# Graph network on one core: setup phases merged, first count-table edges and first feature rows made earlier, issues of weights and x moved

## What is computed

```python
h = maximum(layernorm(x), 0)
feat = einsum('ni,rhid->rnhd', h, conv_weights)             # 8 types: 2048 columns per node
e = leaky_relu(el[type, src] + er[type, dst], 0.2)          # el, er = sum(feat * attn_l / attn_r)
x = x + segment_sum(softmax_per_dst(e) * feat[type, src]) + h_bias
h = maximum(layernorm(x), 0)
h = h @ W_in + b_in
for l in range(3):
    agg = segment_sum(h[src], dst) / deg
    h = relu(agg @ W_agg[l] + h @ W_self[l] + b_hid[l])
x = x + h @ W_out + b_out
```

## Time and profile before

| what | value |
|---|---|
| median of 3 runs | 2069.59 us (2069.22 to 2075.5) |
| the profiled execution: own time, span | 2072.4 us, 2070.6 us |
| busy share of the span | PE 86%, PE weight load 60%, ACT 55%, DVE 52%, POOL 25% |
| mean granted TensorE clock | 0.901 |
| setup, up to the build stage's first one-hot | 0 to 156.6 us |
| build stage, up to the last quarter's store | 156.6 to 529.1 us |
| first gather | 533.0 us |

### The profile page before, as it was taken

The page is one execution under the profiler, slowest core; times in us unless marked ns, Lnnn a source line. Parts: engine busy times, 40 slices in busy tenths (PEclk is TensorE's granted clock), DMA queues, the critical chain, the costliest instruction groups (busy, mean ns, idle before and its releaser), DMA issues. The chain is left out here.

```text
span 2070.6 us, 26209 instructions
## 1 busy us (share of the span) xinstructions
PE 1778.8 (86%) x7604; PEld 1236.5 (60%) x7605; DVE 1081.7 (52%) x3126; ACT 1143.4 (55%) x2498; POOL 521.1 (25%) x544
## 2 busy tenths in 40 slices
PE   1159999999497879798797955999989999999998
PEld 1054444444375557565575634777777777877777
DVE  4858888888365676766767535453550000301011
ACT  0034455565387779797787734454545444544442
POOL 2600000000577777777777300000000000000000
PEclk7569999999687789797898887999999999999999
DMA  4314555555655566565665325333324333363432
GB/s 129 82 14 152 171 195 192 181 201 199 202 146 161 152 182 176 153 188 159 171 173 161 101 63 181 99 123 107 110 77 128 113 116 112 98 208 123 135 123 62
DMA packets 285221, 290.67 MB, mean 140 GB/s; under 512 B 88673, under 2 KB 248102, under 8 KB 284806
## 3 DMA queue, kind: packets, MB, share of 16 engines
q1 hardware_dynamic: 235094, 186.23, 29.3%
q0 software_dynamic: 23952, 66.46, 12.1%
q10 hardware_dynamic: 26016, 36.15, 4.8%
HBM read 201.26 MB, written 87.48 MB: 139 GB/s over the span
## 5 line engine op out<-in xcount | busy, mean ns | idle before, releaser
L1141 POOL DMA_INDIRECT work<-feat_tab,fidx_i x499 | 477.6, 957 | 586.0 <-issue 581.2
L2117 PE MATMUL PS<-a_pe,y_hi 128*128 128x512 f32 (+2 forms) x1440 | 556.7, 392 | 33.4 <-ACT a_pe L2014 33.4
L2117 PE MATMUL PS<-a_pe,y_lo 128*128 128x512 f32 (+2 forms) x1440 | 536.7, 379 | 0.0
L2014 ACT ACTIVATE a_pe<-a_in 128x1536 fp32r<-128x1536 f16 (+1 forms) x240 | 329.3, 1376 | 342.7 <-PE PS L2117 329.1
L2117 PEld LDWEIGHTS PS<-a_pe,y_hi 128*128 128x128 f32 (+1 forms) x1440 | 274.0, 190 | 103.1 <-ACT a_pe L2014 35.0
L1210 ACT ACTIVATE work<-work 128x64 f32<-128x64 f32 x1344 | 325.1, 332 | 0.0
L2117 PEld LDWEIGHTS PS<-a_pe,y_lo 128*128 128x128 f32 (+1 forms) x1440 | 274.2, 190 | 55.2 <-issue 6.7
L1385 PE MATMUL PS<-work,stg 128*128 128x260 f32 x1008 | 289.6, 437 | 6.5 <-ACT work L1210 4.6
L1385 PEld LDWEIGHTS PS<-work,stg 128*128 128x128 f32 x1008 | 207.5, 217 | 65.0 <-issue 19.6
L255 DVE TENSOR_SCALAR side<-iota_c,work 128x512 f16<-128x512 f16 x705 | 245.8, 349 | 0.0
L1325 PE MATMUL PS<-wbuf,hT 128*128 128x512 f32 x480 | 226.9, 595 | 0.0
(11 more groups left out here) (257 smaller groups left out, 1674.0 us busy)
## 6 DMA issues: line engine op xcount, KB each, us to landing
a_in<-a_tab SPq DMA_DIRECT2D x210, 384.0 KB, 3.2
feat_tab<-stg ACTq DMA_DIRECT2D x120, 260.0 KB, 2.2
a_tab<-side SPq DMA_DIRECT2D x235, 128.0 KB, 1.8
stg<-dst_tab SPq DMA_DIRECT2D x42, 384.0 KB, 4.0
work<-feat_tab,fidx_i POOLq DMA_INDIRECT x499
h_tab<-outs SPq DMA_DIRECT2D x42, 130.0 KB, 2.6
h_tab<-outs SPq DMA_DIRECT2D x8, 520.0 KB, 3.9
stg<-h_tab SPq DMA_DIRECT2D x8, 520.0 KB, 4.1
```

The costliest lines, as they stand in the source:

```text
L1141: pool.indirect_dma_start(out=ring[:, s, 0:FE], out_offset=None, in_=feat_tab[:, :], in_offset=bass.IndirectOffsetOnAxis(ap=idx, axis=0)). ...
L2014: act.activation(a_pe[:, load % A_PE, :, 0:n], a_in[:, load % A_IN, :, 0:n], ACT.Copy).then_inc(s_conv, 1)
L2117: mm = pe.matmul(SUMS(ug, n)[:, f, :], y[0:rows_of, kb, f * P:(f + 1) * P], a_pe[0:rows_of, load % A_PE, kb % KB, 0:n], start=(kb == 0 and ...
```

## The change

It has six parts.

- The weights' issues leave the first phase: eight for each half of K, on ACT and on SP, in the phase of tile ends. The attention vectors (ACT) and x with the four small vectors (SP) go into the check phase.
- The products for `wlr` go to the end of the tile tables' lists of DVE and POOL.
- The window phase and the norm phase are one. DVE makes `edge_i` first, behind only the four L749-like instructions and their 28 matmuls, then runs the norm, and then the rest of the window chain. SP starts `load_pairs` when `edge_i` is there, then stores `er_tab`, then `rm_tab`.
- PE and ACT make the 12 quarters of the first `AHEAD` = 3 blocks in this phase, behind the norm.
- The build stage has 27 blocks (3 to 29) for the same 235 windows, so 8 or 9 each; `EARLY` is 8.
- Buffers: the index rows no longer lie in `hT` (an own tile `index_rows`), `hN` and `hTs` lie in `side`, `elr` has its own tile, x's last block is zeroed in the first phase (and again only if a sort ran).

```diff
+AHEAD = 3
+BLOCK_W = [0] * AHEAD + [NREAL * (b + 1) // (NBLK - AHEAD) - NREAL * b // (NBLK - AHEAD) for b in range(NBLK - AHEAD)]
-EARLY = 10
+EARLY = 8
...
+        def load_weights(eng, k):
+            for r in range(R):
+                eng.dma_start(wc[:, k, r * F:(r + 1) * F].rearrange("p (h d) -> p h d", h=H),
+                              conv_w[r, :, k * P:(k + 1) * P, :].rearrange("h p d -> p h d")).then_inc(s_at, 16)
...
+                if flag is None:
+                    @block.scalar
+                    def _(act):
+                        load_weights(act, 0)
+
+                    @block.sync
+                    def _(sp):
+                        load_weights(sp, 1)
...
+            @block.scalar
+            def _(act):
+                load_attention(act)
+
+            @block.sync
+            def _(sp):
+                load_nodes(sp)
...
+                    if flag is None:
+                        attention_sums(dve)
...
+                c.link(dve.tensor_scalar(small[0:1, 35:36], small[0:1, 27:28], float(P), None, ALU.mult))
+                dve.wait_ge(s_we, 1)
+                c.link(dve.tensor_scalar(edge0, PS[0:1, 7, 0:NTW], float(GRAIN), None, ALU.mult))
+                c.link(dve.tensor_scalar(edge0, edge0, small[0:1, 35:36], None, ALU.min))
+                c.link(dve.tensor_copy(edge_i[:, :], edge0))
+                dve.sem_inc(s_wd, 1)
+                dve.wait_ge(s_xr, 1)
+                ln_stats(dve, x_rows(0), 0, 0, s_bs, s_vr)
+                over_chunks(dve, step)
...
                 over_chunks(act, step)
+                act.wait_ge(s_ee, NC)
+                for q in range(4 * AHEAD):
+                    keep_features(act, q)
...
                 halves(NC - 1, (NC - 1) % 2)
+                pe.wait_ge(s_ht, 2 * NC)
+                for cc in range(4):
+                    sum_features(pe, cc)
+                pe.wait_ge(s_ee, NC)
+                for c in range(CT):
+                    pe.matmul(PS[0:1, 5, 0:NTW], one_c, ended[:, PARTS_T - 1, c, :], start=(c == 0), stop=(c == CT - 1))
+                pe.wait_ge(s_w, PARTS_T + 7)
+                for c in range(CT):
+                    mm = pe.matmul(PS[0:1, 6, 0:NTW], ones[:, 0:1], begun[:, c, :], start=(c == 0),
+                                   stop=(c == CT - 1))
+                mm.then_inc(s_wc, 1)
+                for q in range(4, 4 * AHEAD):
+                    sum_features(pe, q)
...
-                for b in range(EARLY):
+                sp.wait_ge(s_wd, 1)
+                for b in range(AHEAD, AHEAD + EARLY):
                     load_pairs(sp, b)
                 over_chunks(sp, store)
+                sp.wait_ge(s_ri, 12)
+                at = 0
+                for a, n in ((csx, U + 1), (cbx, U), (cnx, U)):
+                    for h in range(H):
+                        sp.dma_start(rm_tab[:, at:at + n].unsqueeze(0), a).then_inc(s_rw, 16)
+                        at += n
+                sp.wait_ge(s_rw, 16 * 3 * H)
                 sp.wait_ge(s_et, 16 * NC)
```

More of the change, by code:

```diff
@@ L742, in _, with x_rows, keep, step @@
             def _(dve):
-                dve.memset(x_all[:, NBLK - 1:32, :], 0.0).then_inc(s_xz, 1)
+                def x_rows(c):
+                    return lambda b: x_all[:, bass.ds(c * 4 + b, 1), :].rearrange("p o f -> p (o f)")
+                def keep(c, slot):
+                    dve.wait_ge(s_el, c + 1)
+                    dve.tensor_scalar(elr[:, bass.ds(c * 4, 4), :, :],
+                                      PS[:, 4 + slot, 0:256].rearrange("p (b i n) -> p b i n", b=4, i=2),
+                                      0.0, None, ALU.add).then_inc(s_ee, 1)
+                def step(c, slot, first, last):
+                    if not last:
+                        ln_stats(dve, x_rows(c + 1), c + 1, 1 - slot, s_bs, s_vr)
+                    if not first:
+                        wait_past(dve, s_tp, c - 1)
+                    ln_finish(dve, x_rows(c), c, slot, s_sd, s_rs, s_hn, hN[:, slot, :, :])
+                    if not isinstance(c, int) or c > 1:
+                        keep(c - 2, slot)
+                with when(dve, 0):
+                    dve.memset(x_all[:, FULL:32, :], 0.0).then_inc(s_xz, 1)
                 c = Chain(dve, s_w)
@@ L976, in step @@
                         halves(c - 1, 1 - slot)
+                for g in range(PARTS_T):
+                    pe.wait_ge(s_w, g + 2)
+                    for c in range(CT):
+                        mm = pe.matmul(PS[0:1, 7, 0:NTW], one_c, ended[:, g, c, :], start=(g == 0 and c == 0),
+                                       stop=(g == PARTS_T - 1 and c == CT - 1))
+                mm.then_inc(s_we, 1)
                 over_chunks(pe, step)
                 halves(NC - 1, (NC - 1) % 2)
+                pe.wait_ge(s_ht, 2 * NC)
[5 more added lines that the diff above has]
+                pe.wait_ge(s_w, PARTS_T + 7)
+                for c in range(CT):
+                    mm = pe.matmul(PS[0:1, 6, 0:NTW], ones[:, 0:1], begun[:, c, :], start=(c == 0),
[3 more added lines that the diff above has]
+                    sum_features(pe, q)
             @block.sync
@@ L983, in _ @@
                 sp.wait_ge(s_ld, 16 * 4)
+                sp.wait_ge(s_xl, 32)
+                with when(sp, 0):
+                    load_all_x(sp, 2)
+                    sp.wait_ge(s_xl, 64)
+                sp.sem_inc(s_xr, 1)
                 def store(c, slot, first, last):
@@ L1171, in _ @@
                 w = 0
-                for b in range(NBLK):
+                for b in range(AHEAD, NBLK):
                     for cc in range(4):
-                        q, slot = 4 * b + cc, cc % 2
                         for _ in range(BLOCK_W[b] // 4 + (cc < BLOCK_W[b] % 4)):
@@ L1315, in _ @@
                 w = 0
-                for b in range(NBLK):
+                for b in range(AHEAD, NBLK):
                     for cc in range(4):
-                        q = 4 * b + cc
                         for _ in range(BLOCK_W[b] // 4 + (cc < BLOCK_W[b] % 4)):
```

253 lines of the change are left out of this document (106 added, 147 removed).

## The result

The changed kernel took 2080.94 us (median of 11 runs, 2078.8 to 2091.34); the kernel before took 2074.26 beside it (11 runs, 2063.84 to 2078.3). The ratio is 1.005, with a 95% interval of 1.0032 to 1.0068: it is slower by half a per cent. The forecast of 2054.7, "faster" and the range of 2043 to 2066 are all wrong.

What follows compares the result with a forecast made beforehand. It took setup lists (no engine full) and, in the build stage's loaded part, PE and SP equally full, as the bounds. Gains of 0.9 (setup) and 14 (build stage) made 14.9: span 2055.7, from the median 2054.7 us, range 2043 to 2066.

Steps and rivals of the forecast that it cites:

- the term of the build stage: Build stage: 12 quarters gone and 27 blocks in place of 30, gain taken as 14 us.
- lower bound: Build stage: loaded stretch grows with the windows, 255.1 to 269.8 us; stage 367.6, gain 5.
- upper bound: Build stage: PE sets the pace with the same 14.5 us over, gain 20.5.
- The one for slower: Build stage: longer register loads lengthen SP's list, up to 36.7 us added, 2091; chance 0.04.
- The build stage as the windows go: Build stage at the lower bound, 2064 us; chance 0.15 together with a front 8 us later.
- Quarters at half clock: Merged phase: quarters at 3.42 us in place of 1.71, phase ends with PE, 2072, no change; chance 0.07.
- The lateness goes away: Build stage: pair loads no longer disturb it, 31 us gained, 2038; chance 0.05.
- the four signs of being wrong: Tile ends stretched to 17 us; x's issue held up; merged-phase quarters 3.4 apart; ACT's `a_tab` wait well beyond 57.6.
- First phase and tile ends: Setup: first phase 7.1 us shorter, then eight weight issues on each of ACT and SP, 8.5, end 20.9.
- Check: Setup: SP's issues of x and vectors become the longest list, 11 us (bounds 9.5 and 16), end 31.9.
- Tile tables: Setup: DVE's own 13.7 us as before, then products 16.0, end 66.3, next phase at 68.4.
- Merged phase: Setup: `edge_i` at 81.3, SP's list ends last at 148.4, build stage's first DVE instruction at 153.6, 0.9 us gained.

Runs made afterwards that it cites:

- eight_slots: Changed kernel with eight slots in place of four for window evictions, in a tile of their own: 2249.66 us in one run, build stage 343.2.
- fixed addresses: Changed kernel, pair loads in turn with constant addresses, no register loads (the choice of right edges left out): 2039.71 us in one run, stage 342.8.
- two bursts: Changed kernel with each block's pair loads half at its head, half in its middle: 2045.8 us in one run, stage 345.4.
- in turn: Changed kernel with SP issuing one pair load, one window store, and so on: 2046.75 us, 0.985 of before.
- best: Changed kernel with x's large issue last, loads and stores in turn, POOL's first product held until s_te 6: 2038.68 us, 0.9839 of before.
- interleaved kernel before: Kernel before with pair loads between window stores and nothing else: 2264.45 us, 0.9946 of before on the second chip, stage 361.4.

## Why the prediction was wrong, point by point

**The step that failed: the term of the build stage** ("I take 14", between a lower bound of 5 and an upper of 20.5); the stage grew by 2.8 us where this term took 14 away. It made a sum of SP's list, 250.3, and one of PE's, 237.2, and treated the 14.8 over the sum as a lateness that shrinks.

The sum of SP's list was wrong in itself. Its 0.81 for a window store is the length of a row in which SP also waits for ACT's evictions: 46.8 us of such waits, 48 times, lie in the loaded part of before. Where nothing is waited for, a store comes each 0.50 us (the row of `eight_slots`). By that price the change's list is 166 x 0.50 + 165 x 0.50 + 19 x 2.5 = 213 us, an estimate, and well under PE's 237. SP was not the longer list, and interleaved, the same list let the stage run at PE's pace. What binds is the time in which no window store is issued, against what ACT's slots cover. A quarter with two windows takes 3.01 us, so ACT wants a slot each 1.5 us and four slots are some 6.0 us. This is an estimate; it counts neither the 1.8 us (median) from a store's issue to its landing nor the windows in flight.

The gaps without a store at the blocks' heads, from SP's rows of each trace:

| | gap at a head: median (range) | heads over the cover | cover | stage |
|---|---|---|---|---|
| before | 6.8 (5.0 to 8.7) | 14 of 19 | 6.0 | 372.3 |
| after | 7.7 (5.3 to 10.4) | 16 of 18 | 6.0 | 375.1 |
| fixed addresses | 4.4 (3.9 to 7.1) | 3 of 18 | 6.0 | 342.8 |
| two bursts (the second: 2.7) | 4.9 (3.3 to 7.7) | 6 of 18 | 6.0 | 345.4 |
| in turn | 3.5 (1.7 to 5.4) | none | 6.0 | 344.1 |
| eight slots | 7.9 (5.8 to 10.3) | none | 12.0 | 343.2 |

The four edits work at different places and give the same stage, within 2.6 us: the cause is shown. The 6.0 itself is no sharp edge. With two bursts six heads were over it and PE waited for ACT once, 1.4 us; with fixed addresses three were, and it didn't wait. That goes with the 4 us of ACT's stall that PE does not feel. What gives PE these 4 us, its banks in PSUM ahead of ACT most likely, no run varied. PE's floor by the forecast's own prices is 235 x 0.65 + 108 x 1.71 = 337.4.

The kernel before was already at the edge, and interleaving it gave 11 us. The change took 12 quarters out, but kept every window and made blocks longer: nine loads in a burst in place of eight, and a median gap of 7.7 in place of 6.8. PE's waits for ACT went from 8.4 us to 22.7 by it, as 11 of ACT's 17 stalls were now longer than 4 us (the longest 8.5, before 6.1).

The lower bound was wrong for the same reason: "the stretch goes with the windows" gives 269.8, the profile 278.1. A bound scaled by windows has no term for a burst that gets longer. And of the upper bound, 20.5, the stage without the burst gives 17.3 to 18.8 (361.4 and 362.1 to 344.1 and 343.3), so that number was nearly right, for a kernel in which SP's stores come in time.

**A wrong number in it**: the register load of 1.77 was a median over two phases. Ten of its 30 are in the norm, where they are shorter; the 20 of the stage have a median of 2.32, and 2.55 after the change:

```profile
L215 SPq TENSOR_LOAD <-edge_i x20: 549/2322/3700, 156.8 to 399.1; - x20
```

**The rivals.** The one for slower named SP's list at the block's head, and set its point at a mean register load of 2.55. It was the right place, and the mean in the stage was 2.51; but its working, a sum of extra microseconds added to a list, was that of the failed step, and by it 2.5 would have given no more than "the gain is gone". "The build stage as the windows go" named ACT's waits for SP's stores as what speaks for it: that was the cause, under-weighted. "Quarters at half clock" is refuted for the merged phase: the issues of its quarters come 1.59 to 1.83 apart, but for the gap of 5.56, and the clock was 1.00 from 125 to 153. Half clock came in the build stage, where nobody looked for it, and cost 8 us there. "The lateness goes away" was given 0.05 with the note that SP has more to do per block; it does, and with the loads in turn the lateness goes away all the same. Of the four signs of being wrong two were met: x's issue was held up, and ACT's wait for `a_tab` stores grew to 80.6.

**The setup**, 4.5 us off, as four terms:

- First phase and tile ends: right or better. The landing came 3.0 after the last issue (bounds 2 to 5.7). The 16 issues of weights took 5.8 us on two queues, not 8.5, where one queue had taken 16.92 amid other traffic. But both figures are lengths of issue lists. The pieces landed mostly 0.56 to 0.61 us apart behind the two queues, and the last nine 0.42 to 0.73 apart behind the one of before; the last landing was at 22.67, against 21.16. So the second queue shortened the issue lists, and not the transfers. The Trainium skill says so ("DMA: Bandwidth & Descriptors", section "Issuing engines are not separate DMA queues"): two issuers save only the time to initiate a transfer. The trace agrees; it was the prediction that drew a rival of 17 us for the list from it, and no cost for the transfers left over.
- Check: the mis-sized term, 11 us within bounds of 9.5 and 16; SP's list took 17.8. The 6.44 of x's second issue was measured behind x's first alone, with no other transfer before it; behind the weights and beside the attention vectors it was 14.78, with the last 4.9 us of the weights' transfers in it, and last in the list x holds SP for 5.3 in all. Why the issue behind the large one holds SP in one order and the large one itself in the other isn't known.
- Tile tables: DVE's own part was costed "13.7 as before". It was 17.8, by the 4.2 us that L720 stood beside POOL's product; then the products took 16.0 as forecast. The row says it by itself: 4.60 for an instruction that `best` has at 0.43. The Trainium skill ("SBUF — State Buffer", section "SBUF: two separate sides") has a rule that fits: DVE and GpSimd share a pair of ports as an exclusive lock, held for the whole instruction, and the other fully blocks; for DVE it holds with two SBUF inputs or in a two-port mode. L720 has one input, and whether it ran in such a mode no row tells; its 4.60 agree with a full block. The prediction drew on a neighbouring page and expected "a little".
- Merged phase: from `edge_i` on, SP needed 48.6 us for its loads where 53.4 were forecast, and 1.1 more for its stores; the products, the norm (39.4 for 38.2) and the quarters' pace were right. The count matmuls took 3.7 for 4.7; that fp32 ones cost at most twice the f16 ones was shown by no row, and they took 3.00 against 0.88. The order of the two ends was not right: ACT came 1.4 behind SP, with a gap of 5.56 between the first four quarters and the rest, where the count matmuls stand.

`best`, with x last and POOL held, shows that the front could have given the 7 us and more: the first one-hot at 147.4, against 156.8 before.

## What to carry to other kernels

A burst in an in-order queue is to be set against the buffers behind it, slots times the period of one item, and not added up; where the burst is longer, issue the two kinds in turn or give more slots before anything is taken off the bounding engine. A row of issues that also waits is no price of an issue: look for the queue's waits before you add it up. An issue of thousands of rows goes last in its phase's list, behind the small ones. A POOL instruction moved beside DVE's small ones in SBUF can cost one of them its whole length, and moves the stall with it; place it where DVE reads PSUM.

## What was not expected of the hardware

- An issue of x holds SP's queue 6.44 us with nothing but x in flight, 14.78 behind the weights (332 GB/s moved from 17 to 36), 4.88 as the last of its list.
- Sixteen pieces of 128 KB issued on two queues in 5.8 us landed over 11.5 us from the first issue.
- A stall of ACT of up to 4.1 us cost PE nothing, and each longer one cost it 3.9 to 4.2 us less than its length. Behind PE's stalls of 2.67 us and more the granted clock was down, and the next quarter took 2.94 to 3.33 in place of 1.88.
- A register load on SP takes 0.81 to 3.83 us in the stage where loads and stores are in flight, median 2.55, and 0.54 to 1.87, median 1.25, in the merged phase.
- A DVE instruction of 74 columns took 4.39 us beside a POOL product of 4.50 and 0.26 without it.
- On one of the three chips the part behind the build stage took some 200 us longer for every kernel (span less last issue: 1744.8 for the interleaved kernel before), with the build stage itself unchanged: 344.3 for the same build code on both.
